# A three-part attention and feed-forward kernel: first loads taken apart, job slots and identity fillers changed

## The chip, the cores and the metric

One core of one Trainium2 chip runs the whole program. The metric is device time in microseconds (us), the median of three executions; lower is better. PE is the matmul engine (TensorE), PEld its weight load, DVE the VectorE, ACT the ScalarE, POOL the GpSimd and SP the SyncE, which here issues every transfer.

## The reference, cut to what matters

```python
# x: (4, 2048, 256); 16 heads of 16
x = x + 0.5 * ffn(layernorm(x))          # ffn: x @ W.T + b + (x @ V_r) @ C.T
x = x + attn(layernorm(x))
x = x + 0.5 * ffn(layernorm(x))
# attn
q, k, v = split(x @ W_attn)              # to (B, H, T, 16)
att = q @ k.T / 4, causal, -inf above the diagonal
att = polymax(att)     # x > 0: (x**2 + 1)/1000;  -100 <= x <= 0: (1 - x/100)/1000;  else 0
y = (att @ v) @ W_proj
```

## The kernel before, in words

The 8192 rows are 16 chunks of 512 (`NCH`, `CH`), four to each batch. Attention runs in 16 iterations (`ITERS`): one batch and one quad of four heads each. An iteration has 40 tiles (`TILES`, 128 keys by up to 512 queries), in four windows, one to each 512 queries (c = 0 to 3, of 4, 8, 12 and 16 tiles). A tile is two halves of two heads. PE makes a half's scores into `score`, DVE or ACT raises them into `rp` (and the linear part of a diagonal block into `lin`), POOL and ACT square them, and PE multiplies the tile with `vt` into `y_ps` three tiles later (`LAG`). What lies left of the diagonal for the linear part is one small product per 128 queries, `y_ps<-qT,st`, with a running state `st`; before, it opens a window, ahead of that window's first `values`.

The rest is jobs, in pieces on PE, each emptied from one of two banks by ACT or DVE. Stage A of a chunk: first norm, transposes `z1T`, `ffn`, second norm, transposes `z2T`. Stage B: `qT`, `k`, `v`, transposes `kT`, four `state` products; q and k are then split into three bf16 parts (`parts`, function `split`, on DVE for the first five chunks), stored to DRAM and loaded back into the layout that the score matmuls need. Stage C: `proj`, third norm, transposes `z3T`, `out`.

One line of slots sets the order on every engine: each engine goes through the slots in order and does what is put there. In iterations 1 to 15 each slot has one half, and tables such as `B_FULL` say at which of the iteration's 80 slots a job starts. Ahead of iteration 1 lie six stretches (36, 40, 40, 40, 44 and 48 slots) with stage A of chunk 0, then B of chunk c with A of chunk c + 1; the 80 halves of iteration 0 are spread over the later parts of the last four. I call the stretches S0 to S5 and all of it the warm-up. The slots of the whole warm-up number 248; how long a slot takes depends on what is in it.

Three lines show how the first iteration's inputs were made to wait:

```python
put(x.empty_at + 5, "kq", 0, x.chunk)      # behind the last kT job
all_stored(c + 1)                          # v, qT, parts and state of the chunk in DRAM
load_q(n, c, q_loaded[c]); load_k(n, c, k_loaded[c])
```

## Time and profile before

| what | us |
|---|---|
| median of 3 runs | 1920.25 (1919.88 to 1925.5) |
| the profiled execution, its own time | 1931.65 |
| its span | 1929.9 |
| PE busy | 1665.2 (86%) |
| DVE, ACT, POOL busy | 1361.7, 1363.2, 1326.5 |
| first copy of `y_ps` in iteration 1 | at 314.36 |

The span is what the views below divide up; it lies 1.75 us under that execution's own time. PE has the largest busy share, and its matmuls come at two speeds, which the same group of instructions shows by its duration. A last copy of `y_ps` at 302.28 marks the end of iteration 0, others at 404.86, 508.78 and 611.36 the ends of the next three.

### The profile page before, as it was taken

How to read it: one execution, taken by the hardware profiler on the slowest of the kernel's cores; microseconds unless marked ns; L12 is line 12 of the kernel's file. 1: busy time of each engine (PE TensorE's matmuls, PEld its weight loads, DVE VectorE, ACT ScalarE, POOL GpSimd, SP SyncE). 2: the span in 40 equal slices, each digit the busy share in tenths (PEclk: the TensorE clock that was granted, in tenths of full speed). 3: DMA queues.
4: the chain of work that ended last, by engine and by line, in shares of the span. 5: the costliest groups of instructions: out<-in, count | busy, mean ns of one | idle time of the engine just before them, and what ended most of it. 6: DMA issues, size and time to landing. Idle time of an engine off the chain costs nothing.

```text
span 1929.9 us, 66983 instructions
## 1 busy us (share of the span) xinstructions
PE 1665.2 (86%) x27158; PEld 814.6 (42%) x27158; DVE 1361.7 (71%) x3313; ACT 1363.2 (71%) x2178; POOL 1326.5 (69%) x1419
## 2 busy tenths in 40 slices
PE   4677789898989989898998989898898999898785
PEld 2343334343444435353443535344444444443342
DVE  1465677777777867778786777878676778787672
ACT  1244568787888777777877877777787788888561
POOL 3344558787778868777676877867677767686552
PEclk8888889999999999999999999999999999999897
DMA  2344433241424233341523334241324222323111
GB/s 75 124 128 129 114 106 108 83 110 49 133 67 136 85 103 95 99 132 50 159 66 111 87 106 128 71 135 57 117 86 130 86 72 80 82 73 78 49 37 59
DMA packets 155191, 183.14 MB, mean 95 GB/s; under 512 B 22012, under 2 KB 129660, under 8 KB 152836
## 3 DMA queue, kind: packets, MB, share of 16 engines
q1 hardware_dynamic: 154884, 178.82, 31.6%
q8 instruction: 221, 3.62, 0.8%
q14 instruction: 86, 0.70, 0.1%
HBM read 102.43 MB, written 76.30 MB: 93 GB/s over the span
## 4 chain that ended last, share of the span: by engine, by line
PE 54%; DVE 15%; ACT 12%; issue 8%; POOL 8%; DMA 2%; SPq 0%; ACTq 0%; POOLq 0%; DVEq 0%
PE y_ps L991 20%; PE score L991 16%; PE bank L991 14%; DVE rp L926 9%; ACT rp L831 4%; ACT rp L851 3%; PE bank L1017 3%; POOL rp L735 2%; POOL z L697 2%; ACT rp L847 2%; DVE lin L932 2%; DMA part_scratch<-parts 1%; POOL rp L710 1%; POOL parts L465 1%; DMA x1c<-x_scratch 1%
## 5 line engine op out<-in xcount | busy, mean ns | idle before, releaser
L926 DVE TENSOR_SCALAR rp<-score 128x512 f32<-128x512 f32 (+2 forms) x1728 | 944.1, 573 | 276.0 <-PE score L991 271.3
L991 PE MATMUL score<-qs,ks 96*32 96x512 bf16 (+3 forms) x10240 | 742.7, 354 | 137.8 <-DVE rp L926 74.6
L735 POOL TENSOR_TENSOR rp<-rp 128x1024 f32<-128x1024 f32 (+1 forms) x416 | 756.3, 1830 | 125.1 <-DVE rp L926 114.1
L831 ACT ACTIVATE rp<-score 128x512 f32<-128x512 f32 (+1 forms) x832 | 458.4, 592 | 267.8 <-PE score L991 266.2
L991 PE MATMUL y_ps<-rp,vt 128*16 128x512 f32 (+3 forms) x5120 | 597.8, 537 | 24.3 <-ACT rp L851 13.3
L991 PEld LDWEIGHTS score<-qs,ks 96*32 96x32 bf16 x10240 | 294.4, 96 | 547.9 <-DVE rp L926 266.8
L847 ACT ACTIVATE rp<-rp,rise 128x1024 f32<-128x1024 f32 (+1 forms) x416 | 462.6, 1144 | 1.7 <-POOL rp L710 1.7
L710 POOL TENSOR_SCALAR_AFFINE_SELECT rp<-rp 128x256 f32<-128x256 f32 (+1 forms) x384 | 185.2, 484 | 317.2 <-DVE rp L926 161.5
L851 ACT ACTIVATE rp<-rp 128x1024 f32<-128x1024 f32 (+2 forms) x224 | 291.1, 1305 | 131.4 <-DVE rp L926 66.0
L932 DVE SCALAR_TENSOR_TENSOR lin<-score,slope_mask 128x128 f32<-128x128 f32 x768 | 214.4, 279 | 0.0
L991 PEld LDWEIGHTS y_ps<-rp,vt 128*16 128x16 f32 x5120 | 134.4, 97 | 111.5 <-ACT rp L851 25.7
L991 PE MATMUL bank<-w_ffn,zT 128*32 128x256 f32 x2048 | 160.3, 401 | 5.4 <-ACT zT L791 5.4
L991 PE MATMUL bank<-w_qkv,z2T 128*32 128x256 f32 x2048 | 152.5, 388 | 11.2 <-ACT parts L808 11.2
L1017 PE MATMUL bank<-ident,z 128*128 128x128 f32 x384 | 72.7, 327 | 45.2 <-POOL z L697 42.9
L991 PE MATMUL y_ps<-lin,vt 128*16 128x128 f32 x2048 | 106.2, 276 | 0.0
L991 PEld LDWEIGHTS bank<-w_ffn,zT 128*32 128x32 f32 x2048 | 69.0, 115 | 79.6 <-issue 51.6
L697 POOL TENSOR_SCALAR z<-x,rstd_ln,shift_ln 128x256 f32<-128x256 f32 x128 | 72.6, 575 | 40.8 <-DVE shift_ln L885 39.3
L991 PEld LDWEIGHTS y_ps<-lin,vt 128*16 128x16 f32 x2048 | 61.5, 97 | 80.0 <-issue 67.8
L991 PEld LDWEIGHTS bank<-w_qkv,z2T 128*32 128x32 f32 x2048 | 67.3, 112 | 62.4 <-issue 28.0
L991 PE MATMUL bank<-w_out,y_c 128*32 128x256 f32 x1024 | 83.4, 400 | 11.8 <-DMA x1c<-x_scratch 11.8
L1017 PEld LDWEIGHTS bank<-ident,z 128*128 128x128 f32 x384 | 49.6, 164 | 88.5 <-issue 78.2
L697 POOL TENSOR_SCALAR z<-x_sb,rstd_ln,shift_ln 128x256 f32<-128x256 f32 x64 | 35.0, 558 | 68.2 <-DVE shift_ln L885 68.2
(78 smaller groups left out, 1360.0 us busy)
## 6 DMA issues: line engine op xcount, KB each, us to landing
part_scratch<-parts SPq DMA_DIRECT2D x16, 1536.0 KB, 7.5
qs<-part_scratch SPq DMA_DIRECT2D x384, 64.0 KB
ks<-part_scratch SPq DMA_DIRECT2D x384, 64.0 KB, 2.4
state_scratch<-st_new SPq DMA_DIRECT2D x16, 528.0 KB
st<-state_scratch SPq DMA_DIRECT2D x64, 132.0 KB
x_sb<-in_L_attn_x_dram SPq DMA_DIRECT2D x16, 512.0 KB, 4.4
x_scratch<-x SPq DMA_DIRECT2D x16, 512.0 KB, 5.4
qT_scratch<-qkT SPq DMA_DIRECT2D x16, 512.0 KB, 3.8
```

The lines of the kernel that those rows point to most:

```text
L465: ins = eng.tensor_tensor(parts[:, i, 2, :], rest[:], parts[:, i, 1, :], ALU.subtract)
L697: ins = pool.tensor_scalar(dst[:, i, :], src[:, i, :], rstd[k][:, i:i + 1], shift[k][:, i:i + 1], ALU.mult, ALU.add)
L710: pool.affine_select(out=block, in_=block, compare_op=ALU.is_ge, fill=fill, base=0, pattern=[[0, heads_in_it], [1, P]], channel_multiplier ...
L735: pool.tensor_tensor(half, half, half, ALU.mult).then_inc(squared["pool"], 1)
L831: nc.scalar.activation(rp[T % RP_BUFS][:, 2 + v, off:CH], score[H % S_BUFS][:, v, off:CH], ACT.Relu).then_inc(raised["act"], 1)
L847: nc.scalar.activation(part, part, ACT.Square, bias=rise[:]).then_inc(squared["act"], 1)
L851: nc.scalar.activation(whole, whole, ACT.Square).then_inc(squared["act"], 1)
L926: nc.vector.tensor_scalar(rp[T % RP_BUFS][:, 2 * u + v, off:CH], score[H % S_BUFS][:, v, off:CH], 0.0, RISE, ALU.max, ALU.add).then_inc(ra ...
L932: nc.vector.scalar_tensor_tensor(lin[D % L_BUFS][:, 2 * u + v, :], score[H % S_BUFS][:, v, off:off + P], ONE / SLOPE, slope_mask[:, 0, :], ...
L991: return nc.tensor.matmul(*args, start=start, stop=stop, skip_group_check=True)
L1017: ins = nc.tensor.transpose(dst[:, P * blk:P * blk + P], src[:, blk, P * i:P * i + P], ident[:])
```

## The change

Eight things are edited.

- Slots: the warm-up's stretches are 36, 40, 42, 39, 44 and 48 slots; halves of window c begin 33, 31, 31 and 33 slots into stretches S1 to S4 and are spread until the next window's begin. In stage B `kT` goes ahead of `v` and right behind `k`; the tables of the later iterations shift by 1 to 5 slots (`kT` part two from 52 to 57, `state` from 54, 56, 58 to 59, 61, 63).
- First transfers: for the first four chunks the half of q and the half of k that hold quad 0 are stored by themselves as soon as they are split, and quad 0 is loaded at once; v and the state's q go from SBUF to SBUF; the state is loaded late. The other halves of q and k follow in one store behind `kT`.
- `load_q` and `load_k` load only q and k; v, qT and the state have functions, semaphores and waits of their own.
- The state product closes a window instead of opening it, in pieces of 16 columns in place of 32, and the accumulation is started by the first `rp` product.
- Start: x is loaded first, four fills (`st_new`, `k_sb`, `qT`, `y_sb`) move from POOL to DVE, which also clears both `y_ps` banks, engines wait for the constants and weights that they need and not for all.
- Norms: ACT adds EPS as a bias of the square root, and the DVE addition is gone; the wait for the previous `z` moves to `aggregate`.
- Fillers: ahead of the transposes `z1T` and `z2T` of chunks 0 to 4, and of `proj` and `z3T` of the last chunk, PE does 48 matmuls of the identity by itself (12 times 4 strips of 128 columns) into the bank that the job is about to fill.
- Buffers freed in that way are waited for in `empty`.

```diff
-A_EARLY = {"z1T": (12, 13), "ffn": (14, 18), "z2T": (38, 39), "ln1": 0, "ln2": 22}
-B_EARLY = {"qT": (0, 2), "k": (4, 8), "v": (22, 26), "kT": (30, 32), "state": (31, 33, 34, 35)}
+A_EARLY = {"z1T": (12, 13), "ffn": (16, 20), "z2T": (38, 39), "ln1": 0, "ln2": 24}
+B_EARLY = {"qT": (4, 6), "k": (7, 8), "kT": (14, 15), "v": (26, 28), "state": (34, 35, 36, 37)}
+FILLERS = 12
+FILLED_UP = {(kind, c) for kind in ("z1T", "z2T") for c in range(CPB + 1)} | {("proj", NCH - 1), ("z3T", NCH - 1)}
+HALVES_AFTER = (33, 31, 31, 33)
+LENGTHS = (36, 40, 42, 39, 44, 48)
...
-    for c, (length, first) in enumerate(((40, 20), (40, 14), (44, 14), (48, 14))):
-        at = o.stretch(length, spread(first, length, 2 * (LAST[c] + 1 - FIRST[c])))
+    for c, length in enumerate(LENGTHS[1:]):
+        at = o.stretch(length)
+        o.stage(c, at, B_EARLY)
+        o.stage(c + 1, at, A_EARLY)
+        if c < CPB:
+            starts.append(at + HALVES_AFTER[c])
+    starts.append(o.n)
+    for c in range(CPB):
+        o.put_halves(spread(starts[c], starts[c + 1], 2 * (LAST[c] + 1 - FIRST[c])))
...
+                    if what == "first q":
+                        wait_emptied(sp, "qT", c, 0)
+                        sp.dma_start(qT[1:QD + 1, cols], qkT[0:QD, 0, :]).then_inc(qT_loaded[c], 16)
+                        sp.wait_ge(split_step, 12 * c + 3)
+                        sp.dma_start(part_d[c, :, 0, 0], parts[:, 0, :, :]).then_inc(first_q_stored, 16)
+                        sp.wait_ge(first_q_stored, (c + 1) * 16)
+                        load_q(0, c, q_loaded[c])
+                    if what == "first k":
+                        sp.wait_ge(split_step, 12 * c + 9)
+                        sp.dma_start(part_d[c, :, 1, 0], parts[:, KC, :, :]).then_inc(first_k_stored, 16)
+                        sp.wait_ge(first_k_stored, (c + 1) * 16)
+                        load_k(0, c, k_loaded[c])
...
-            act.wait_ge(const_ready, CONSTS)
+            def empty_weights():
...
+                if s == o.place["z1T", 0, 0].empty_at:
+                    empty_weights()
...
-            dve.wait_ge(const_ready, CONSTS)
+            nc.vector.memset(eps[:], EPS)
+            for k in range(KC):
+                nc.vector.memset(y_ps[k][:], 0.0).then_inc(y_cleared, 1)
+            nc.vector.memset(st_new[:], 0.0).then_inc(filled, 1)
+            nc.vector.memset(k_sb[:], 1.0).then_inc(filled, 1)
+            nc.vector.memset(qT[:], 1.0).then_inc(filled, 1)
+            nc.vector.memset(y_sb[0][:], 0.0).then_inc(filled, 1)
...
-                nc.vector.tensor_scalar(var[k][:], mv[k][:, :, 1], EPS, None, ALU.add).then_inc(var_done[k], 1)
...
+                if first and (kind, a) in FILLED_UP:
+                    for _ in range(FILLERS):
+                        strips(dst[:, 0:P], ident[:], ident[:])
...
-                    for m in range(NB):
-                        strips(y[:, P * m:P * m + P], st[:, NB * c + m, :], qT[:, CH * c + P * m:CH * c + P * m + P],
-                               start=m == 0, stop=False)
...
+                if t == LAST[c]:
+                    pe.wait_ge(qT_loaded[c], (n + 1) * 16)
+                    pe.wait_ge(st_loaded[c], (n + 1) * 16)
+                    for m in range(NB):
+                        for head in range(QH):
+                            ins = mm(y[STRIP * head:STRIP * head + HD, P * m:P * m + P],
+                                     st[:, NB * c + m, STRIP * head:STRIP * head + HD],
+                                     qT[:, CH * c + P * m:CH * c + P * m + P], start=False, stop=m == NB - 1)
```

On SP's queue, this is the stretch from the first qT store to the loads of chunk 0's q and k, before (`z` and `rp` above it hold weights at the start; `qkT`, `v_sb`, `st_new` and `parts` are the results that are stored):

```order
L595 DMA qT_scratch<-qkT 128x2x512
L590 DMA x_sb<-in_L_attn_x_dram 128x4x256
L591 DMA x_scratch<-x 128x4x256
L599 DMA v_scratch<-v_sb 128x1024
L608 DMA part_scratch<-parts 128x6144
L603 DMA state_scratch<-st_new 66x4x512
L516 DMA qs<-part_scratch 16x4x512 x6
L518 DMA qT<-qT_scratch 64x512
L521 DMA st<-state_scratch 66x4x128
L505 DMA ks<-part_scratch 16x4x512 x6
```

and the same place of the changed kernel:

```order
L668 DMA qT<-qkT 64x512
L670 DMA part_scratch<-parts 128x1536
L546 DMA qs<-part_scratch 16x4x512 x6
L642 DMA qT_scratch<-qkT 128x2x512
L676 DMA part_scratch<-parts 128x1536
L531 DMA ks<-part_scratch 16x4x512 x6
L660 DMA part_scratch<-parts 256x1x1536
L637 DMA x_sb<-in_L_attn_x_dram 128x4x256
L638 DMA x_scratch<-x 128x4x256
L646 DMA v_scratch<-v_sb 128x1024
L682 DMA vt<-v_sb 128x256
```

The loads of q and k now stand ahead of the next chunk's x, of the v store and of the state store; a quarter of `parts` goes out ahead of each.

On PE, this is the place where the very first half of iteration 0 stands, before:

```order
L1017 MATMUL bank<-ident,z 128x128 x8
L991 MATMUL bank<-w_ffn,zT 32x256 x24
L991 MATMUL score<-qs,ks 32x512 x8
L991 MATMUL bank<-w_ffn,zT 32x256 x8
L991 MATMUL score<-qs,ks 32x512 x8
```

and the same place of the changed kernel, with the filler of chunk 1's second transposes behind it:

```order
L1084 MATMUL bank<-w_ffn,zT 32x256 x32
L1084 MATMUL bank<-w_qkv,z2T 32x256 x32
L1084 MATMUL score<-qs,ks 32x512 x8
L1084 MATMUL bank<-v_sb,k_sb 32x64 x2
L1084 MATMUL bank<-v_sb,k_sb 2x64
L1084 MATMUL bank<-v_sb,k_sb 32x64 x2
...
L1084 MATMUL bank<-v_sb,k_sb 32x64 x2
L1084 MATMUL bank<-v_sb,k_sb 2x64
L1084 MATMUL bank<-v_sb,k_sb 32x64 x2
L1084 MATMUL bank<-v_sb,k_sb 2x64
L1084 MATMUL bank<-ident 32x128 x48
L1110 MATMUL bank<-ident,z 128x128 x8
```

The first half stood in the `ffn` of chunk 2; now it stands behind the `v` of chunk 0, one whole stretch earlier, ahead of the state products of chunk 0 and of the filler and the transposes of chunk 1.

Also on PE, the turn from one window to the next, in the warm-up: before,

```order
L991 MATMUL y_ps<-rp,vt 16x128 x4
L991 MATMUL y_ps<-lin,vt 16x128 x4
L991 MATMUL bank<-w_ffn,zT 32x256 x4
L991 MATMUL score<-qs,ks 32x512 x8
L991 MATMUL bank<-w_ffn,zT 32x256 x4
L991 MATMUL score<-qs,ks 32x512 x8
L991 MATMUL y_ps<-qT,st 32x128 x16
```

and now

```order
L1084 MATMUL score<-qs,ks 32x512 x8
L1084 MATMUL y_ps<-rp,vt 16x128 x4
L1084 MATMUL y_ps<-lin,vt 16x128 x4
L1084 MATMUL y_ps<-qT,st 16x128 x16
L1084 MATMUL score<-qs,ks 32x512 x16
L1084 MATMUL y_ps<-rp,vt 16x512 x4
```

The state product is 16 matmuls in both. It has moved up by two halves, and belongs to the window that ends.

## Rows read from the trace of the kernel before

**Rows 1.** The page: span, and busy time of each engine.

```profile
span 1929.9 us, 66983 instructions
PE 1665.2 (86%) x27158; PEld 814.6 (42%) x27158; DVE 1361.7 (71%) x3313; ACT 1363.2 (71%) x2178; POOL 1326.5 (69%) x1419
```

**Rows 2.** Stretches: length, busy PE, PEld, DVE, ACT, POOL, granted clock, DMA share, GB/s.

```profile
0.00:24.70 24.70, 6.89 (x20) 4.44 (x21) 2.30 (x11) 4.18 (x7) 10.67 (x24) 1.00 0.35 104
...
39.70:72.10 32.40, 24.26 (x344) 13.51 (x344) 13.49 (x39) 9.27 (x18) 8.25 (x14) 0.84 0.22 67
72.10:113.00 40.90, 30.92 (x456) 17.45 (x457) 23.82 (x60) 14.33 (x29) 17.59 (x25) 0.83 0.42 134
113.00:164.00 51.00, 37.99 (x608) 20.45 (x608) 30.13 (x80) 22.15 (x41) 24.53 (x32) 0.89 0.39 123
164.00:218.50 54.50, 42.67 (x652) 20.98 (x648) 34.14 (x84) 28.46 (x48) 26.10 (x30) 0.91 0.37 115
218.50:302.30 83.80, 70.60 (x1000) 32.14 (x1000) 59.19 (x134) 50.90 (x82) 43.45 (x47) 0.84 0.43 126
302.30:404.90 102.60, 92.15 (x1565) 44.32 (x1561) 78.12 (x189) 83.55 (x136) 79.97 (x83) 1.00 0.32 94
...
957.80:1069.90 112.10, 100.95 (x1704) 49.36 (x1700) 83.98 (x203) 85.18 (x139) 84.94 (x91) 0.98 0.34 102
1600.90:1691.50 90.60, 81.92 (x1359) 37.43 (x1352) 70.51 (x171) 75.16 (x117) 65.94 (x67) 1.00 0.29 77
```

**Rows 3.** Timeline of the start: begin, duration, instruction, idle time before and releaser.

```profile
12.26 0.40 PE L1003 MATMUL score<-ident,rp 128*32 128x128 f32 x1 [12.26 <-POOL bias_half L684]
...
22.40 2.17 POOL L697 TENSOR_SCALAR z<-x_sb,rstd_ln,shift_ln 128x256 f32<-128x256 f32 x4 [10.19 <-DVE shift_ln L885]
...
24.71 1.94 PE L1017 MATMUL bank<-ident,z 128*128 128x128 f32 x8 [4.84 <-POOL z L697]
...
27.43 6.34 PE L991 MATMUL bank<-w_ffn,zT 128*32 128x256 f32 x64 [0.78 <-ACT zT L791]
...
39.66 1.94 PE L1017 MATMUL bank<-ident,z 128*128 128x128 f32 x8 [5.88 <-POOL z L697]
```

**Rows 4.** Timeline of PE's queue in the warm-up.

```profile
55.23 1.06 PE L1017 MATMUL bank<-ident,z 128*128 128x128 f32 x8 [3.71 <-POOL z L697]
...
62.09 3.64 PE L991 MATMUL bank<-w_qkv,z2T 128*32 128x256 f32 x64
65.67 0.66 PE L1050 MATMUL bank<-ident,k_sb 128*128 128x128 f32 x4
66.54 0.64 PE L991 MATMUL bank<-v_sb,k_sb 128*32 128x64 f32 x24 [0.22 <-ACT v_sb L798]
...
98.20 0.62 PE L991 MATMUL score<-qs,ks 96*32 96x512 bf16 x8
```

**Rows 5.** Timeline of SP's queue and of ACT, 75 to 90 us.

```profile
75.24 0.36 SPq L608 DMA_DIRECT2D part_scratch<-parts  x1
...
83.31 2.70 SPq L516 DMA_DIRECT2D qs<-part_scratch  x6
...
81.70 0.60 ACT L807 ACTIVATE qkT<-bank 128x512 f32<-128x512 f32 x1 [7.78 <-DMA part_scratch<-parts]
```

**Rows 6.** DMA issues on the page: KB each and median us to landing.

```profile
qT_scratch<-qkT SPq DMA_DIRECT2D x16, 512.0 KB, 3.8
y_scratch<-y_sb SPq DMA_DIRECT2D x256, 32.0 KB, 1.7
```

**Rows 7.** Groups by form, iteration from 957.8 to 1069.9: count, busy us, mean ns, idle before.

```profile
L926 DVE TENSOR_SCALAR rp<-score 128x512 f32<-128x512 f32 x68 | 43.6, 682 | 7.1 <-PE score L991 6.9
...
L991 PE MATMUL score<-qs,ks 96*32 96x512 bf16 x448 | 37.5, 386 | 8.9 <-DVE rp L926 5.3 <-DVE lin L932 3.4
...
L991 PE MATMUL y_ps<-qT,st 66*32 66x128 f32 x128 | 4.2, 272 | 0.0
```

**Rows 8.** Timeline of the end.

```profile
1900.93 6.55 PE L991 MATMUL bank<-w_out,y_c 128*32 128x256 f32 x64 [6.08 <-DMA x1c<-x_scratch]
```

More of the change, by code:

```diff
@@ L155, in stage, with put_halves @@
                 self.jobs.append(Job(kind, chunk, i, at + start))
+    def put_halves(self, slots):
+        for s in slots:
+            assert s not in self.halves
+            self.halves[s] = self.next_half
+            self.next_half += 1
     def stretch(self, length, slots=()):
-        for s in slots:
-            self.halves[self.n + s] = self.next_half
-            self.next_half += 1
+        self.put_halves([self.n + s for s in slots])
         at = self.n
@@ L364, in build @@
         bank = [ps(f"bank{i}", [P, CH]) for i in range(2)]
-        w_loaded = sem("w_loaded")
+        ffn_loaded = sem("ffn_loaded")
+        bias_loaded = sem("bias_loaded")
+        qkv_loaded = sem("qkv_loaded")
+        out_loaded = sem("out_loaded")
+        ident_ready = sem("ident_ready")
+        filled = sem("filled")
+        y_cleared = sem("y_cleared")
+        first_q_stored = sem("first_q_stored")
+        first_k_stored = sem("first_k_stored")
         const_ready = sem("const_ready")
@@ L393, in build @@
         q_loaded = [sem(f"q_loaded{c}") for c in range(CPB)]
+        v_loaded = [sem(f"v_loaded{c}") for c in range(CPB)]
+        qT_loaded = [sem(f"qT_loaded{c}") for c in range(CPB)]
+        st_loaded = [sem(f"st_loaded{c}") for c in range(CPB)]
         qk_done = sem("qk_done")
@@ L569, in _ @@
                     put(x.empty_at + (2 if x.chunk < EARLY else 8), "parts", x.chunk)
-                    if x.chunk < CPB:
-                        put(x.empty_at + 5, "kq", 0, x.chunk)
+                if x.chunk < CPB:
+                    if (x.kind, x.i) == ("qT", 0):
+                        put(x.empty_at + 2, "first q", x.chunk)
+                    if (x.kind, x.i) == ("kT", 0):
+                        put(x.empty_at + 2, "first k", x.chunk)
+                    if (x.kind, x.i) == ("v", 1):
+                        put(x.empty_at + 1, "first v", x.chunk)
+                    if (x.kind, x.i) == ("state", NB - 1):
+                        put(x.empty_at + 7, "first st", x.chunk)
                 if (x.kind, x.i) == ("proj", 0):
@@ L615, in slot @@
+                    if what == "first st":
+                        c, = args
+                        sp.wait_ge(st_zero, 16 * BATCH)
+                        sp.wait_ge(st_stored, (c + 1) * 16)
+                        load_st(0, c, st_loaded[c])
                     if what == "q":
@@ L779, in _ @@
             nc.scalar.activation(cT[:], score[0][0:32, 0, DM:2 * DM], ACT.Copy).then_inc(setup_act, 1)
-            for k in range(KC):
-                act.wait_ge(setup_pe, 2 + k)
-                nc.scalar.activation(w_ffn[:, k, :], y_ps[k][:, 0:DM], ACT.Copy, scale=0.5).then_inc(setup_act, 1)
-            act.wait_ge(const_ready, CONSTS)
+            def empty_weights():
+                for k in range(KC):
+                    act.wait_ge(setup_pe, 2 + k)
+                    nc.scalar.activation(w_ffn[:, k, :], y_ps[k][:, 0:DM], ACT.Copy, scale=0.5).then_inc(setup_act, 1)
+                act.wait_ge(const_ready, CONSTS)
+                act.wait_ge(filled, FILLED)
             def empty(x):
@@ L858, in slot @@
                     if step == ROOT:
-                        act.wait_ge(var_done[k], chunk + 1)
-                        nc.scalar.activation(sd[k][:], var[k][:], ACT.Sqrt).then_inc(sd_done[k], 1)
+                        act.wait_ge(aggr_done[k], (chunk + 1) * NB)
+                        nc.scalar.activation(sd[k][:], mv[k][:, :, 1], ACT.Sqrt, bias=eps[:]).then_inc(sd_done[k], 1)
             for s in range(o.again):
+                if s == o.place["z1T", 0, 0].empty_at:
+                    empty_weights()
                 slot(s)
@@ L957, in _ @@
             for s in range(o.again):
+                if s == o.place["z1T", 0, 0].empty_at:
+                    dve.wait_ge(const_ready, CONSTS)
                 slot(s)
@@ L1035, in job @@
                         pe.wait_ge(c_loaded, (a + 1) * 32)
+                    if first and kind == "ffn" and a == 0:
+                        pe.wait_ge(setup_act, 4)
+                    if first and kind == "proj" and a == 0:
+                        pe.wait_ge(out_loaded, 16)
                     if first and kind in ("ffn", "out"):
@@ L1042, in job @@
                 if kind == "qT":
+                    if first and a == 0:
+                        pe.wait_ge(qkv_loaded, 16)
                     if first:
@@ L1098, in values @@
                     ins = mm(y[STRIP * head:STRIP * head + HD, off:CH], vt[:, kb, HD * head:HD * head + HD],
-                             rp[T % RP_BUFS][:, head, off:CH], start=False, stop=t == LAST[c])
+                             rp[T % RP_BUFS][:, head, off:CH], start=t == FIRST[c], stop=False)
                 if t in DIAG:
```

139 lines of the change are left out of this document (80 added, 59 removed).

## The prediction

> **What bounds the kernel now.** I read the page first: PE is busy 86% of the span, the other three 69 to 71% [rows 1], so PE's order and what it waits for decide. Then the stretches [rows 2]. Three kinds of time stand out. From 302.3 us on the kernel runs at a steady beat: 102.6 us for an iteration with stages A and B beside it, 112.1 with C as well, 90.6 with attention alone, and PE busy about 90% of each. The warm-up is another matter: from 39.7 to 302.3, 262.6 us, PE is busy only 75, 76, 74, 78 and 84% of the five stretches, and part of that is time at the lower clock: the granted clock there has means of 0.83 to 0.91, against 0.98 to 1.00 later. The third is the start, 24.7 us until the first transposes.
>
> In the start, every engine waits for POOL's work on the bias, which itself waits for the last weight: PE's first matmul is at 12.26. The first z is ready at 24.6, and the same eight transposes and the 64 products behind them take 1.94 and 6.34 us [rows 3], where later they take 1.06 and 3.64 [rows 4]. In the warm-up the timeline shows why PE is idle: no half may come until q, k, v and the state of the chunk are all stored and loaded, so the first score is at 98.20 [rows 4], 23 us behind the store of parts at 75.24, whose landing SP's loads (83.31) and ACT's next qT (7.78 us idle) both wait for [rows 5]. Until then PE has one chain to work on and nothing to fill its gaps; later the halves come in bunches between gaps.
>
> **The start.** x comes first, so the norm no longer waits for 12.2. DVE has its fills first: 6672 elements per partition over six. No row has a DVE fill. The bounds are nothing, if x lands behind them, and 9 us, at the 0.68 us that DVE takes to raise 512 columns of scores [rows 7]. A fill reads nothing, so I take 7, nearer to the upper end, and begin the statistics at 8. The Trainium skill (VectorE: DVE Perf Modes, "Zero memsets can be issued as uint32 (trn2)") says that a memset takes one cycle per element, which at the 0.96 GHz that the page gives is an estimate of 7.0 us; by it the term stays as it is. Then statistics and scales 4, POOL 2.2 [rows 3]: z at about 14. PE's twenty weight products are 6.89 us of its time [rows 2] with one step of ACT between; begun at 8 instead of 12.26, they end at 16. Then comes the filler. It is 96 records of 128 columns, where the 64 of 256 took 3.64: 2.7 us at the higher clock, and by 6.34 for 64, 4.8 at the lower. So the transposes start at 19 to 21 instead of 24.7. The 64 products behind them then run at the higher clock (2.7 less), and chunk 0's second transposes come at 32 instead of 39.7 (29 to 36): 7.7 gained.
>
> Why should a filler lift the clock? The rows give it: behind an idle gap of 5.88 the eight transposes take 1.94 [rows 3], behind one of 3.71 only 1.06 [rows 4]. A filler of 2.7 in a gap of 5.9 leaves 3.2. The Trainium skill (TensorE: Matmul & The Clock Gate, "What's actually happening") says the same in general, that the lower level is the default and activity releases it. Against it speaks Part 4 of that page, "PE-mode transpose", by which transposes don't count as such activity: if that held here, a filler which is followed only by transposes could be worth less, and each of the first four would cost its time and give back nothing.
>
> **The warm-up.** The same work in another order, so I sum it in two ways.
>
> First, by marginal price. Stages A and B of one chunk are PE work of four blocks of 3.64 (qT, k, v, ffn), two kT at 0.66, four state products at 0.64, and two sets of transposes at 1.06 [rows 4]: 20.5 us. C is some 8.3 (two blocks and one set of transposes) and adds 112.1 - 102.6 = 9.5 [rows 2], 1.13 for 1. An iteration with one A and B is 102.6, four more are 4 x 20.5 x 1.13 = 93, together 195. To that come S1, which has one half and cannot be filled (30 rather than 23: 7), six fillers in S2 to S4 at 2.7, of which I charge two thirds (11), and the splits, which in the warm-up are DVE's (3). Sum 216.
>
> Second, by PE's share. S1 to S5 have 24.26 + 30.92 + 37.99 + 42.67 + 70.60 us of PE, times their clocks 178 at the higher level [rows 2]; eight fillers add 22; at the 90% of an iteration that is 222. I take 219 between them, and iteration 0 ends at 32 + 219 = 251 instead of 302.3: 51 us less.
>
> Is q and k there in time? The kT of chunk 0 is now made some 11 slots before v is. Its split is 2.5 us of DVE, the store of 384 KB lands in 1.7 to 3.8 (32 KB and 512 KB, [rows 6]), SP then issues six loads in 2.7 [rows 5], and they land some 2 later (by the smaller of [rows 6]): about 11 us from kT to the first half, where PE has ffn and v, 7.3 us. So PE waits some 4 us at the first half, and the four state products and the second transposes of chunk 1 wait behind it. This is in S1's 30. Later stretches have halves of the window before in that place, and the wait is covered; without that cover it would be 4 us for each of three. SP itself stands still while it waits for each small store; behind it are the next x load and the stores of v and the state, needed a dozen slots later, so I cost that at nothing. If they came late, the next norm would be late by the same 2 to 4 us.
>
> **Later iterations.** The state product costs what it did, 4.2 us of records in an iteration [rows 7], with as many matmuls on as many columns, and moves past one tile's scores: nothing. DVE loses one small operation in each norm, and the shifted jobs spread what DVE and ACT empty over slots 49 to 63, where PE's 8.9 us of waiting for DVE in an iteration mostly lie [rows 7]. A gain is at most these 8.9 and a loss has no row as its bound; eleven iterations have such jobs. I take 0 for the likeliest, between -10 and +10 in all.
>
> **The end.** The last proj follows a gap of 6.08 us and takes 6.55 rather than 3.64 [rows 8]. Its filler lies in the gap: 2.9 gained if the clock holds, and about as much at z3T and out; at most 1 lost. I take 3.
>
> **Sum.** 51 + 3 = 54 us off the profiled 1931.65, so 1878 for that execution. It was 11.4 above the median of the runs; I carry the same difference, which gives 1920.25 - 54 = 1866.
>
> **Rivals.**
> (a) The warm-up fills badly. DVE has the splits and maxima there, halves stand in the order's way, the fillers delay scores instead of filling gaps, or each window's first half waits for its loads. For it: DVE has 59.19 us in the last stretch before and PE waits for it already. Against it: even then DVE is at 71% [rows 2]. If S2 to S5 reach only the 78% that PE had from 164 on, instead of 90, 200/0.78 = 256 us in place of 219, and the gain is 17: 1903. The page's rule on transposes, as a mechanism, comes in here: fillers without effect cost 2.7 each and leave the lower clock, 3.6 us for each of the four early sets, and the gain falls by some 20: 1886.
> (b) The later iterations gain as well. If the spread of the emptying takes 2.5 of the 8.9 us out of each of eleven, 28 more: 1838.
> (c) Slower. The shifted slots put state 61 and z2T 61 into one slot, both z3T into slot 69, and v with proj into 22 and 23, so PE waits for a bank to be emptied while DVE is behind in raising. It decides when it costs more than 54/11 = 4.9 us per iteration; at 6 it is 66, and 1932. Against it: the pairs alternate between the two banks and most gaps around them are of PE's making.
> (d) It does not do what it says: the first half waits for something that still comes at 90 us, for example in S1 for a blocked SP. Then only the start and the end are left, some 11 us: 1909.
>
> **How the numbers follow.** The forecast has 0.68, with a range of its own from 1845 to 1886; (a) 0.15, (b) 0.07, (c) 0.06, (d) 0.04. 1866 is the time of the first. The range leaves out (c) and half of (b): 1838 to 1902. Within 0.3% (6 us) is about what a measurement cannot tell from no change; only edges of (c) and (d) lie there, so same has 0.03, slower 0.05, faster 0.92.
>
> **What the profile after would show.** Right: PE's first matmul at 7 to 9 us, the second transposes of chunk 0 near 32, the first score at 55 to 60, the fourth copy of y_ps (end of iteration 0) near 251, a granted clock above 0.95 from 70 us on, and iterations still of 102 to 104 and 111 to 113 us. Wrong: the fourth copy after 270 with PE waiting for DVE's rp or for loads of q and k, transposes of 1.9 us behind fillers, or an iteration of more than 114.

## The result, and the profile after

The changed kernel takes 1789.11 us, the median of four runs (1787.53 to 1792.33), against 1922.88 (1919.88 to 1926.72) for the kernel before on the same chip: a ratio of 0.9305 [0.928, 0.9331]. The forecast was 1866, with a range down to 1838; the gain is 134 us where 54 were expected. The profiled execution took 1787.62.

The page after, span and busy time of each engine (compare [rows 1]):

```profile
span 1785.9 us, 69303 instructions
PE 1636.3 (92%) x28310; PEld 866.6 (49%) x28310; DVE 1327.8 (74%) x3272; ACT 1363.1 (76%) x2178; POOL 1318.3 (74%) x1415
```

The stretches after, with the columns of [rows 2]:

```profile
0.00:19.60 19.60, 11.33 (x117) 8.49 (x117) 7.95 (x17) 4.27 (x7) 8.54 (x23) 1.00 0.44 132
...
31.00:64.90 33.90, 27.53 (x553) 17.18 (x553) 18.20 (x46) 10.59 (x22) 10.91 (x18) 0.95 0.44 141
64.90:101.70 36.80, 31.52 (x667) 21.20 (x664) 27.07 (x66) 16.95 (x33) 20.57 (x29) 1.00 0.51 157
101.70:148.80 47.10, 41.77 (x853) 24.90 (x849) 33.34 (x77) 24.10 (x40) 25.37 (x28) 0.96 0.46 143
148.80:201.40 52.60, 46.14 (x836) 25.48 (x834) 35.19 (x84) 30.87 (x50) 27.54 (x32) 0.97 0.35 114
201.40:265.90 64.50, 55.18 (x897) 27.42 (x900) 48.58 (x109) 42.63 (x71) 37.09 (x43) 0.97 0.35 111
265.90:361.20 95.30, 90.26 (x1568) 45.20 (x1564) 75.02 (x188) 83.69 (x136) 79.60 (x83) 1.00 0.35 103
868.70:970.00 101.30, 97.48 (x1708) 52.07 (x1700) 80.07 (x201) 85.45 (x140) 84.87 (x92) 1.00 0.37 109
```

The end of iteration 0 moved from 302.3 to 265.9: 36.4 us, where I had forecast 51. Iterations 1 to 11 went from 102.6 to 95.3 us each without C and from 112.1 to 101.3 with it, 102.6 us in all, where I had forecast nothing. The rest (iterations 12 to 15 and the end) gave 5. So the larger half of the gain lies in a place that I had priced at 0, and PE is now busy 95 and 96% of such an iteration, not 90.

The timeline of PE's start after, with the columns of [rows 3]:

```profile
7.54 0.37 PE L1096 MATMUL score<-ident,rp 128*32 128x128 f32 x1 [7.54 <-DMA z<-in_L_ffn_W_dram]
...
15.06 4.60 PE L1084 MATMUL bank<-ident 128*32 128x128 f32 x96
19.59 1.09 PE L1110 MATMUL bank<-ident,z 128*128 128x128 f32 x8
21.60 3.66 PE L1084 MATMUL bank<-w_ffn,zT 128*32 128x256 f32 x64 [0.92 <-ACT zT L871]
25.05 2.83 PE L1084 MATMUL bank<-ident 128*32 128x128 f32 x96
30.93 1.09 PE L1110 MATMUL bank<-ident,z 128*128 128x128 f32 x8 [3.04 <-POOL z L774]
...
58.30 0.62 PE L1084 MATMUL score<-qs,ks 96*32 96x512 bf16 x8 [1.43 <-DMA ks<-part_scratch]
```

The start is as I drew it: first matmul at 7.54, a filler of 4.60 and then one of 2.83 (so the clock of 1.00 given for the first stretch cannot be right: the durations decide), transposes of 1.09 and 64 products in 3.66 behind it, second transposes at 30.93, first score at 58.30. On SP's queue the small store of k and the loads of chunk 0 stand so close together:

```profile
50.20 0.37 SPq L676 DMA_DIRECT2D part_scratch<-parts  x1
53.02 2.68 SPq L531 DMA_DIRECT2D ks<-part_scratch  x6
```

DVE's fills took this long (two of its six rows of fills):

```profile
1.15 1.02 DVE L958 MEMSET y_ps<- 128x512 f32 x2
2.59 1.76 DVE L959 MEMSET st_new<- 66x2048 f32 x1 [0.41 <-issue]
```

### The profile page after: what moved, and what is told of

Read it like the earlier page. It is cut to its first block, busy times and chain, and to the rows that moved or that the text cites. A ratio compares the mean times of both kernels' runs of the same rounds, so it can differ in the third digit from the quotient of the medians.

```text
span 1785.9 us, 69303 instructions
## 1 busy us (share of the span) xinstructions
PE 1636.3 (92%) x28310; PEld 866.6 (49%) x28310; DVE 1327.8 (74%) x3272; ACT 1363.1 (76%) x2178; POOL 1318.3 (74%) x1415
## 4 chain that ended last, share of the span: by engine, by line
PE 59%; DVE 15%; ACT 11%; issue 6%; POOL 5%; DMA 2%; SPq 2%; ACTq 0%; POOLq 0%; DVEq 0%
PE y_ps L1084 21%; PE bank L1084 18%; PE score L1084 16%; DVE rp L1017 9%; ACT rp L915 4%; PE bank L1110 3%; ACT rp L931 2%; POOL rp L812 2%; DVE lin L1023 2%; DMA x1c<-x_scratch 2%; ACT rp L935 1%; DVE bnst_ln L1042 1%; ACT lin L921 1%; POOL z L774 1%; SPq L531 1%
## 5 line engine op out<-in xcount | busy, mean ns | idle before, releaser
L1084 PE MATMUL score<-qs,ks 96*32 96x512 bf16 (+3 forms) x10240 | 729.4, 350 | 54.0 <-DVE lin L1023 22.4
L915 ACT ACTIVATE rp<-score 128x512 f32<-128x512 f32 (+1 forms) x832 | 463.1, 602 | 210.3 <-PE score L1084 208.1
L1084 PEld LDWEIGHTS score<-qs,ks 96*32 96x32 bf16 x10240 | 306.2, 96 | 431.6 <-DVE rp L1017 142.7
L1084 PEld LDWEIGHTS y_ps<-rp,vt 128*16 128x16 f32 x5120 | 143.8, 96 | 117.4 <-issue 38.9
L1084 PE MATMUL bank<-w_ffn,zT 128*32 128x256 f32 x2048 | 154.8, 387 | 4.5 <-ACT zT L871 2.9
L1084 PEld LDWEIGHTS y_ps<-lin,vt 128*16 128x16 f32 x2048 | 65.1, 96 | 74.3 <-issue 62.4
L1084 PE MATMUL bank<-w_out,y_c 128*32 128x256 f32 x1024 | 88.5, 390 | 13.1 <-DMA x1c<-x_scratch 13.1
L921 ACT ACTIVATE lin<-score 128x128 f32<-128x128 f32 x256 | 80.7, 315 | 0.0
L1110 PE MATMUL bank<-ident,z 128*128 128x128 f32 x384 | 61.0, 292 | 19.5 <-POOL z L774 18.7
L1084 PE MATMUL bank<-z2T,w_qkv 128*32 128x512 f32 x512 | 68.1, 605 | 2.3 <-ACT z2T L871 2.3
```

Of the source, the lines that this page charges most:

```text
L915: nc.scalar.activation(rp[T % RP_BUFS][:, 2 + v, off:CH], score[H % S_BUFS][:, v, off:CH], ACT.Relu).then_inc(raised["act"], 1)
L921: nc.scalar.activation(lin[D % L_BUFS][:, 2 + v, :], score[H % S_BUFS][:, v, off:off + P], ACT.Copy, scale=SLOPE, bias=ONE).then_inc(lin_d ...
L1084: return nc.tensor.matmul(*args, start=start, stop=stop, skip_group_check=True)
L1110: ins = nc.tensor.transpose(dst[:, P * blk:P * blk + P], src[:, blk, P * i:P * i + P], ident[:])
```

## Where the later iterations' time went: DVE standing still in three places

I had read DVE by its busy share. These are groups by form of DVE in the kernel before, in the iteration of [rows 7] (957.8 to 1069.9): count, busy, mean ns, idle before them and what ended it.

```profile
L885 DVE SCALAR_TENSOR_TENSOR shift_ln<-mv_ln,rstd_ln 128x4 f32<-128x4 f32 x3 | 3.8, 1278 | 0.1
L912 DVE TENSOR_TENSOR st_add<-bank,smask 66x256 f32<-66x256 f32 x4 | 1.7, 421 | 3.6 <-PE bank L991 2.2 <-POOL st_new L759 1.5
L903 DVE SCALAR_TENSOR_TENSOR x<-bank,x1c 128x512 f32<-128x512 f32 x2 | 1.4, 692 | 3.2 <-PE bank L991 3.2
L897 DVE TENSOR_TENSOR x<-bank,x_sb 128x512 f32<-128x512 f32 x2 | 1.4, 692 | 1.4 <-PE bank L991 1.3
L908 DVE TENSOR_TENSOR x<-bank,x 128x512 f32<-128x512 f32 x2 | 1.4, 692 | 4.1 <-PE bank L991 4.1
```

And the same groups after, 868.7 to 970.0:

```profile
L976 DVE SCALAR_TENSOR_TENSOR shift_ln<-mv_ln,rstd_ln 128x4 f32<-128x4 f32 x3 | 1.8, 616 | 0.1
L1003 DVE TENSOR_TENSOR st_add<-bank,smask 66x256 f32<-66x256 f32 x4 | 1.7, 415 | 1.1 <-PE bank L1084 1.1
L994 DVE SCALAR_TENSOR_TENSOR x<-bank,x1c 128x512 f32<-128x512 f32 x2 | 1.4, 692 | 1.9 <-PE bank L1084 1.9
L999 DVE TENSOR_TENSOR x<-bank,x 128x512 f32<-128x512 f32 x2 | 1.4, 692 | 1.5 <-PE bank L1084 1.5
L988 DVE TENSOR_TENSOR x<-bank,x_sb 128x512 f32<-128x512 f32 x2 | 1.4, 692 | 0.8 <-PE bank L1084 0.8
```

DVE raises two thirds of the scores (1728 of the 2560 pieces on the page), in order with all else that it does. Whatever holds it there holds the next scores on PE. Three things held it: the idle time ahead of emptying a `state` product (3.6 us, now 1.1), that ahead of emptying `proj`, `ffn` and `out` (3.2 + 1.4 + 4.1 = 8.7, now 4.2), and `shift_ln`, an operation on four elements that took 3.8 us in three (now 1.8). Together 16.1 before and 7.1 after: 9.0 of the 10.8 us by which this iteration is shorter. The first two are idle time of an engine that was not the bound by its share, the third counts as busy. In iteration 2, summed in the same way, it is 9.0 and 3.9, 5.1 of the 8.7. Over iterations 1 to 11 the three come to 155.6 us before and 66.8 after, where the length fell by 102.5.

A part of the gain is the clock: its mean was 0.98 in six of iterations 1 to 11 before, and 1.00 in all eleven after. It is not the main part: in the kernel of experiment 17 it was 1.00 in all eleven too, and they took 71 us more than in the changed kernel.

**Emptying ahead of raising.** A job's last piece is emptied by DVE in the slot where PE computes it, ahead of that slot's raising. In an even slot PE has the scores of a half, then a whole tile's `values`, and then the piece. This is the kernel before in such a slot, a timeline of PE and DVE:

```profile
471.15 0.40 PE L991 MATMUL score<-qs,ks 96*32 96x512 bf16 x4 [0.40 <-DVE lin L932]
471.37 1.04 PE L991 MATMUL y_ps<-rp,vt 128*16 128x512 f32 x8
472.23 0.52 PE L991 MATMUL bank<-v_sb,k_sb 128*32 128x64 f32 x18
472.90 0.42 DVE L912 TENSOR_TENSOR st_add<-bank,smask 66x256 f32<-66x256 f32 x1 [1.31 <-PE bank L991]
473.25 0.68 DVE L926 TENSOR_SCALAR rp<-score 128x512 f32<-128x512 f32 x1
473.98 0.40 PE L991 MATMUL score<-qs,ks 96*32 96x512 bf16 x4 [0.69 <-DVE rp L926]
```

The scores that end at 471.55 are raised only from 473.25 on: DVE idles for 1.31 us until the product is there, which stands behind them and behind the values, empties it, and PE then waits 0.69 us for DVE. In an odd slot there are no values and it is mostly ACT that raises; here is the changed kernel with a state product in such a slot:

```profile
425.30 0.61 PE L1084 MATMUL score<-qs,ks 96*32 96x512 bf16 x8
425.73 0.51 PE L1084 MATMUL bank<-v_sb,k_sb 128*32 128x64 f32 x18
425.81 1.14 ACT L915 ACTIVATE rp<-score 128x512 f32<-128x512 f32 x2
426.41 0.42 DVE L1003 TENSOR_TENSOR st_add<-bank,smask 66x256 f32<-66x256 f32 x1 [0.61 <-PE bank L1084]
426.46 1.18 PE L1084 MATMUL y_ps<-rp,vt 128*16 128x512 f32 x8
```

The tables moved `state` from slots 48, 54, 56, 58 to 49, 59, 61, 63, and the emptying of `out` from 74 and 78 to 75 and 79. `proj` and `ffn` were emptied in odd slots before and are still; that the idle time ahead of them fell too (3.2 to 1.9 and 1.4 to 0.8) is not explained by the kind of slot.

**An operation of four elements held by POOL.** `shift_ln` takes 0.2 us when it is alone. In the kernel of experiment 1 (the changed one with the old tables) it takes 3.31 and ends at 435.65; the product's last matmul ended at 435.17, so here it is `shift_ln` that keeps the emptying and the raise behind it waiting:

```profile
431.89 3.74 POOL L812 TENSOR_TENSOR rp<-rp 128x1024 f32<-128x1024 f32 x2
432.34 3.31 DVE L976 SCALAR_TENSOR_TENSOR shift_ln<-mv_ln,rstd_ln 128x4 f32<-128x4 f32 x1
432.82 1.05 PE L1084 MATMUL score<-qs,ks 96*32 96x512 bf16 x16
433.70 1.03 PE L1084 MATMUL y_ps<-rp,vt 128*16 128x512 f32 x8
434.56 0.50 PE L1084 MATMUL bank<-v_sb,k_sb 128*32 128x64 f32 x18
435.58 0.41 DVE L1003 TENSOR_TENSOR st_add<-bank,smask 66x256 f32<-66x256 f32 x1
435.91 0.67 DVE L1017 TENSOR_SCALAR rp<-score 128x512 f32<-128x512 f32 x1
```

POOL had begun two squarings at 431.89 and ends at 435.63. This is the rule, not a coincidence: in the twenty kernels of this study 607 executions of `shift_ln` took over 0.25 us, and every one began while POOL was at work and ended within 0.03 us of the end of a POOL operation, typically 0.02 behind it. Most of them met a squaring of `rp`; 49 met only POOL's selects (0.4 us), and were 0.25 to 0.42 us long. The other 353 took 0.16 to 0.25 us, and where one of them began beside a POOL operation, that had at most 0.24 us left. It can sit through several in a row. The kernel of experiment 16, with C, shows it at its worst; POOL, DVE and PE in one timeline:

```profile
937.11 3.74 POOL L812 TENSOR_TENSOR rp<-rp 128x1024 f32<-128x1024 f32 x2
937.30 4.69 DVE L976 SCALAR_TENSOR_TENSOR shift_ln<-mv_ln,rstd_ln 128x4 f32<-128x4 f32 x1
939.20 0.63 PE L1084 MATMUL score<-qs,ks 96*32 96x512 bf16 x8
940.82 1.15 POOL L492 TENSOR_TENSOR parts<-rest,parts 128x512 bf16<-128x512 f32 x1
941.91 0.68 DVE L1017 TENSOR_SCALAR rp<-score 128x512 f32<-128x512 f32 x1
942.93 0.62 PE L1084 MATMUL score<-qs,ks 96*32 96x512 bf16 x4 [3.10 <-DVE lin L1023]
```

POOL's three operations end at 941.97, DVE's at 941.99, and PE then has waited 3.10 us. `shift_ln` is DVE's only operation in these iterations that reads two tensors from SBUF; all the others, which read PSUM or one tensor, keep their usual length (the raise of 512 columns is never over 0.69 us in iterations 1 to 11 of the changed kernel, `lin` never over 0.29). The Trainium skill (SBUF — State Buffer, "SBUF: two separate sides") gives a reason: a DVE operation with two SBUF inputs and a GpSimd operation that reads SBUF take turns at a shared pair of ports for the whole instruction, and the loser fully blocks. The traces agree, with 0.2 us alone and up to 4.69 behind POOL.

## The experiments

The ratio is against the kernel before on the same chip, whose median was 1922 to 1928 us beside the different experiments; compare by it rather than by the times. The last columns are the mean length of an iteration without C (1 to 3) and with it (4 to 10), first score to first score.

| run | median us | ratio [95%] | without C | with C |
|---|---|---|---|---|
| kernel before | 1922.88 | 1 | 103.0 | 111.6 |
| changed kernel | 1789.11 | 0.9305 [0.928, 0.9331] | 95.3 | 101.2 |
| 1 old tables | 1896.12 | 0.9834 [0.9817, 0.985] | 103.5 | 111.4 |
| 2 old norm | 1798.58 | 0.9331 [0.9311, 0.935] | 95.8 | 101.5 |
| 3 state opens | 1782.62 | 0.9244 [0.9228, 0.9259] | 95.6 | 100.4 |
| 4 no fillers | 1782.35 | 0.9248 [0.9226, 0.9269] | 95.3 | 101.3 |
| 5 only B table | 1866.55 | 0.9713 [0.9685, 0.9741] | 98.6 | 109.3 |
| 6 only state | 1861.13 | 0.968 [0.9655, 0.9705] | 100.9 | 107.5 |
| 7 only kT | 1866.82 | 0.9707 [0.968, 0.9734] | 100.5 | 108.3 |
| 8 four st_add | 1873.38 | 0.9754 [0.9721, 0.9787] | 102.1 | 109.0 |
| 9 before, new tables | 1822.13 | 0.9485 [0.9459, 0.9512] | 95.5 | 100.7 |
| 10 both of 3 and 4 | 1775.08 | 0.9244 [0.9219, 0.9269] | 95.1 | 100.1 |
| 11 only A table | 1876.73 | 0.9768 [0.9744, 0.9791] | 101.0 | 109.1 |
| 12 old warm-up slots | 1805.91 | 0.9401 [0.9361, 0.9441] | 95.3 | 101.2 |
| 13 short POOL split | 1879.37 | 0.976 [0.9741, 0.9779] | 101.4 | 109.7 |
| 14 short DVE | 1887.23 | 0.9795 [0.9777, 0.9812] | 102.7 | 109.6 |
| 15 short ACT | 1877.93 | 0.9758 [0.9738, 0.9778] | 101.2 | 109.2 |
| 16 A and B tables | 1839.19 | 0.9563 [0.9533, 0.9592] | 95.3 | 106.8 |
| 17 state odd, close | 1866.45 | 0.97 [0.9673, 0.9727] | 101.3 | 108.0 |
| 18 state even, spread | 1886.49 | 0.9802 [0.9781, 0.9823] | 102.4 | 110.0 |

**1. The changed kernel with the old tables.**

```diff
-A_FULL = {"z1T": (32, 33), "ffn": (36, 40), "z2T": (61, 63), "ln1": 10, "ln2": 45}
-B_FULL = {"qT": (0, 7), "k": (8, 12), "v": (16, 20), "kT": (45, 57), "state": (49, 59, 61, 63)}
-C_FULL = {"proj": (22, 26), "ln3": 30, "z3T": (69, 69), "out": (72, 76)}
+A_FULL = {"z1T": (32, 34), "ffn": (38, 42), "z2T": (61, 63), "ln1": 8, "ln2": 45}
+B_FULL = {"qT": (0, 6), "k": (8, 12), "v": (16, 20), "kT": (46, 52), "state": (48, 54, 56, 58)}
+C_FULL = {"proj": (24, 28), "ln3": 32, "z3T": (65, 67), "out": (71, 75)}
```

> The changed kernel with the job tables of the later iterations (A_FULL, B_FULL, C_FULL) as before; warm-up, norms, state product and fillers stay. Theory 1 (the shifted jobs of iterations 1 to 11 gave the 103 us that these iterations gained): about 1875 to 1890, with an iteration back at 102 us without C and 112 with C. Theory 2 (the norm without its DVE addition and with its wait moved) and theory 3 (the state product at the window's end): within 10 us of the changed kernel's 1789.

Measured: 107 us slower than the changed kernel by the times, 102 by the ratios, and its iterations are nearly those of the kernel before. The three tables carry the whole of the later gain.

**2. The norm as before.**

```diff
-                        nc.scalar.activation(sd[k][:], mv[k][:, :, 1], ACT.Sqrt, bias=eps[:]).then_inc(sd_done[k], 1)
+                        nc.scalar.activation(sd[k][:], var[k][:], ACT.Sqrt).then_inc(sd_done[k], 1)
...
+                nc.vector.tensor_scalar(var[k][:], mv[k][:, :, 1], EPS, None, ALU.add).then_inc(var_done[k], 1)
```

> The changed kernel with the norm as before: DVE adds EPS in an operation of its own that waits for the four aggregates, and the wait for the previous z stands ahead of the reciprocal. Theory 2: 1860 or more, since DVE's wait inside the norm would stop the raising of scores behind it. Theory 1 and 3: 1789 to 1797, three small operations per iteration.

Measured: 0.9331, its interval overlaps that of the changed kernel. At most a few us, if anything. In its one profile iteration 1 begins at 264.3 instead of 257.3, and iterations 1 to 11 take 3.6 us more in all.

**3. The state product at the opening of a window, from iteration 1 on.**

```diff
-                if t == LAST[c]:
+                if t == LAST[c] and n == 0:
...
+                if t == FIRST[c] and n > 0:
```

> The changed kernel with the state product at the opening of a window, in pieces of 32 columns, as before, in iterations 1 to 15 (iteration 0 keeps it at the end). Theory 3: 1850 or more. Theory 1 and 2: 1785 to 1795; the attention-only iterations say that the place is worth under 1 us each (91.4 after against 90.6 before).

Measured: about 0.6% faster by the ratio, 6.5 us by the times. From iteration 1 on, closing a window with the state product costs some 0.4 to 0.8 us in an iteration. "Nothing", as I had it, was a small error of the other sign. Whether it helps in iteration 0, where the state comes late, no run shows: this kernel has it at the end there too.

**4. No fillers.**

```diff
-FILLERS = 12
+FILLERS = 0
```

> The changed kernel without fillers. My sum charged eleven us for them in the warm-up against 2.7 to 3.6 given back at each of the first sets and 3 at the end: 1780 to 1800. If they lift the clock for long stretches, 1810 or more, with transposes of 1.9 us at 19, 31 and 45 us; if they only cost, 1775.

Measured: also about 0.6% faster by the ratio, 6.8 us by the times. The kernel without fillers, timeline of its start and of its end:

```profile
15.23 1.97 PE L1110 MATMUL bank<-ident,z 128*128 128x128 f32 x8
17.97 6.00 PE L1084 MATMUL bank<-w_ffn,zT 128*32 128x256 f32 x64 [0.78 <-ACT zT L871]
...
1752.19 5.88 PE L1084 MATMUL bank<-w_out,y_c 128*32 128x256 f32 x64 [7.69 <-DMA x1c<-x_scratch]
```

The fillers do what they are said to: with them the same lines take 1.09, 3.66 and, at the end, 5.02. But transposes and ffn of chunk 0 begin at 15.23 and not at 19.59, which pays for both, and each later filler costs 2.8 in a stretch where PE is short of time: iteration 1 begins at 248.4 without them and at 257.3 with them. At the end they give 1.9 us from proj to the last matmul (21.07 to 19.15).

**9. The kernel before with the three new tables and nothing else.**

```diff
-B_FULL = {"qT": (0, 6), "k": (8, 12), "v": (16, 20), "kT": (46, 52), "state": (48, 54, 56, 58)}
+B_FULL = {"qT": (0, 7), "k": (8, 12), "v": (16, 20), "kT": (45, 57), "state": (49, 59, 61, 63)}
```

(A_FULL and C_FULL likewise.)

> The kernel before with the three tables of the later iterations new (A_FULL, B_FULL, C_FULL) and nothing else. If the tables do the same without the rest of the change: 1922 - 107 = 1815 (1808 to 1825), iterations of 95.3 and 101. If they need the norm without its addition, or the state product at the window's end: 1840 or more.

Measured: 1822.13, 100 us under the kernel before. Neither the norm nor the place of the state product is needed for it.

**10. Experiments 3 and 4 together.**

> The changed kernel without fillers and with the state product at the opening of a window in iterations 1 to 15: each alone was 11 us faster than the changed kernel by its ratio. If they add: ratio 0.918 to 0.921, about 1767. If both do the same thing (PE's work in the same places): 0.924.

Measured: 1775.08, the fastest kernel here, 14 us under the changed one. By ratio it is level with each of the two alone; the kernel before ran at 1922 beside it and at 1928 beside them, so the ratios do not tell whether the two gains add.

**12. The warm-up's slots of before, with the new stores and start.**

```diff
-LENGTHS = (36, 40, 42, 39, 44, 48)
+    for c, (length, first) in enumerate(((40, 20), (40, 14), (44, 14), (48, 14))):
```

(and A_FIRST, A_EARLY and B_EARLY of before.)

> The changed kernel with the warm-up's slots as before (stretches, places of the halves, A_FIRST, A_EARLY, B_EARLY); the first stores, the start and the fillers stay new. If the earlier and evenly spread halves give the warm-up's gain: the first score at 80 or later, the end of iteration 0 at 290 or more, and 1805 to 1820. If the smaller first stores and the start are the gain: 1789 to 1797.

Measured: 1805.91, and iteration 1 begins at 272.7, where the changed kernel has 257.3 and the one before 293.7. The first score falls back to 84.59, and iteration 0 ends at 281.3, not at 290. So the slots are worth 15 us of the 36, and the start, the stores apart and the fillers the other 21; each of my two cases had one of them alone.

**5, 11, 16, 6 and 7. One table, two tables, one row of a table.** From experiment 1: only the new B_FULL; only the new A_FULL; both; only `state` at 49, 59, 61, 63; only `kT` at 45 and 57. The edits of the last two:

```diff
-"state": (48, 54, 56, 58)
+"state": (49, 59, 61, 63)
...
-"kT": (46, 52)
+"kT": (45, 57)
```

> The changed kernel with A_FULL and C_FULL as before, so that of the three tables only B_FULL (qT, kT, state) is new. Theory 1a (the crowd in slots 46 to 60, where kT, four state products, the splits on POOL and the second norm meet, is what was relieved): most of the 107 us stay, 1800 to 1825. Rival 1b (ffn, z1T, proj, norms and out matter as much): 1840 to 1870.

> The changed kernel with B_FULL and C_FULL as before, only A_FULL new (z1T, ffn and the first norm of the iteration). B_FULL alone gave 23 of 107 us. If the parts help only together, because each of them takes work out of slots 44 to 60 and the slowest of the others remains: 1870 to 1890. If A alone has the missing 80: 1815 to 1830.

> The changed kernel with A_FULL and B_FULL new and C_FULL as before. In iterations without C: 95.3 as in the changed kernel. With C: if A and B add up as they do without it (2 and 2 us alone), 107, ratio 0.955; if C's own shift matters little, 102 and 0.935.

> All three tables old, but the state products at 49, 59, 61, 63 instead of 48, 54, 56, 58. If the state products' chain (PE, DVE, POOL's addition, next DVE) is what stops PE behind DVE: 1825 to 1850. If kT's second part with its splits is: 1880 to 1896.

> All three tables old, but kT at 45 and 57 instead of 46 and 52. State chain theory: 1880 to 1896. kT and splits theory (ACT's two copies, POOL's two subtractions of 1.16 us away from slots 54 and 55): 1825 to 1850.

Measured: by the ratios, of the 102 us, 13 with A alone, 23 with B alone, 52 with both, so they do not add. `state` alone and `kT` alone each give as much as all of B (0.968 and 0.9707 against 0.9713). That is a miss of both theories of 6 and 7: each had one of the two doing nearly all and the other next to nothing. In the traces `kT` seems to work through `shift_ln`: in iteration 2 the longer of its two executions takes 0.34 us, where experiment 1 has 3.31, while the idle time ahead of the emptied `state` products even rises, from 4.4 to 5.0, and the iteration falls from 103.6 to 100.5 (a part of that is the clock, 0.97 and 1.00). Experiment 16 separates C: without C its iterations are those of the changed kernel (95.3), with it they are 5.6 longer. The groups by form of DVE in its iteration 868.6 to 975.7:

```profile
L976 DVE SCALAR_TENSOR_TENSOR shift_ln<-mv_ln,rstd_ln 128x4 f32<-128x4 f32 x3 | 5.3, 1770 | 0.1
...
L999 DVE TENSOR_TENSOR x<-bank,x 128x512 f32<-128x512 f32 x2 | 1.4, 692 | 4.1 <-PE bank L1084 4.1
```

`shift_ln` takes 3.5 us more than in the changed kernel, and the two emptyings of `out`, here in even slots, have 2.6 more idle time ahead of them: 6.1, in an iteration that is 6.2 longer, first score to first score. Here C's table is worth what these two say.

**8. Four buffers for `st_add`**, with the old tables.

```diff
-        st_add = [sb(f"st_add{i}", [QR, DM]) for i in range(2)]
+        st_add = [sb(f"st_add{i}", [QR, DM]) for i in range(4)]
...
-                    if a * NB + i >= 2:
+                    if a * NB + i >= 4:
```

> All three tables old, with four st_add buffers instead of two, so that DVE does not wait for POOL's addition before it masks the next state product. If DVE's wait for POOL (1.5 us of idle in the iteration's trace) with the raising of scores queued behind it is the mechanism: 1840 to 1875. If POOL's and DVE's own load in these slots is: 1885 to 1896.

Measured: 0.9754, by the ratio 15 us under experiment 1. POOL's part of the wait (1.5 us before) can be taken away so, and is the smaller part.

**13, 14 and 15. Is it too much work rather than its order?** With the old tables, each leaves work out on one engine.

> The changed kernel with the old tables (as e1_old_tables, ratio 0.983) where POOL's two subtractions of each split, 1.16 us each, are done on 8 columns instead of 512 in iterations 1 to 15, so that work is left out and the output is not the reference's. POOL theory (in slots 48 to 60 POOL is the engine that holds everybody up): the iterations fall to 96 to 98 without C, ratio 0.94 to 0.95. Rival theories (ACT, or DVE itself): ratio 0.97 to 0.98.

> The changed kernel with the old tables where DVE's masking of the state products and its maxima of q and k work on 8 columns in iterations 1 to 15 (3.6 us of DVE less per iteration, work left out). DVE theory: ratio 0.945 to 0.955. POOL theory: 0.97 to 0.98.

> The changed kernel with the old tables where ACT's part of the splits and its two copies of kT work on 8 columns in iterations 1 to 15 (4.8 us of ACT less per iteration, work left out). ACT theory: ratio 0.945 to 0.955. POOL theory: 0.97 to 0.98.

Measured: 0.976, 0.9795 and 0.9758, so 4 to 8 parts in a thousand, where the order of the jobs is worth 53. The load that these edits take away is not the cause, on any of the three engines. In the first, the shorter splits also change when POOL's work meets `shift_ln`, which falls from 3.3 to 2.3.

**17 and 18. Odd or even, close or spread.** With the old tables, `state` alone at other slots:

```diff
-"state": (48, 54, 56, 58)
+"state": (49, 55, 57, 59)    # 17
+"state": (50, 60, 62, 64)    # 18
```

> All three tables old, state products at 49, 55, 57, 59 instead of 48, 54, 56, 58: one slot later each, spacing as before. In an even slot PE does a half's scores, then a tile's values, then the state product, and DVE empties that product before it raises the same half; in an odd slot there are no values and mostly ACT raises. Parity theory: at least two thirds of e6's 30 us, ratio 0.968 to 0.975. Spacing theory (the products must be spread and come later): 0.980 to 0.984.

> All three tables old, state products at 50, 60, 62, 64: spread and late as in e6 (49, 59, 61, 63), but in even slots. Parity theory: little of e6's gain, ratio 0.978 to 0.984. Spacing theory: ratio 0.966 to 0.972.

Measured, as a square: even and close 0.9834, odd and close 0.970, even and spread 0.9802, odd and spread 0.968. Odd slots gain 0.012 to 0.013 either way, spreading 0.002 to 0.003. Ahead of the four emptyings in iteration 2 DVE is idle for 4.4, 3.0, 7.5 and 2.6 us in that order. Even and spread has 3 us more of it than even and close and is still not slower, because its `shift_ln` meets POOL at another moment: 0.6 us, against 3.3.

**What the square left open, as the traces have it.** Here is what DVE stands for in iteration 7, in the three places, beside the iteration's length:

| kernel | shift_ln | idle ahead of st_add | ahead of proj, ffn, out | sum | iteration |
|---|---|---|---|---|---|
| before | 3.8 | 3.6 | 8.8 | 16.2 | 112.1 |
| 1 | 4.2 | 3.8 | 7.6 | 15.6 | 110.3 |
| 5 | 5.8 | 1.1 | 7.6 | 14.5 | 109.5 |
| 18 | 1.5 | 6.8 | 7.6 | 16.0 | 109.5 |
| 11 | 4.5 | 3.8 | 7.7 | 16.0 | 108.5 |
| 7 | 3.6 | 3.0 | 7.6 | 14.2 | 108.3 |
| 6 | 4.5 | 2.4 | 6.8 | 13.7 | 107.5 |
| 16 | 5.3 | 1.1 | 7.7 | 14.1 | 107.1 |
| changed | 1.8 | 1.1 | 4.2 | 7.1 | 100.9 |
| 3 | 1.6 | 1.1 | 3.4 | 6.1 | 100.2 |

Over all twenty kernels the sum and the length go together with a correlation of 0.98 in iteration 7 and 0.94 in iteration 2, at 0.95 and 1.12 us of iteration per us of standing. Much of that is two groups, seven kernels that stand 6.0 to 7.2 us in iteration 7 and thirteen that stand 13.7 to 16.2; among the thirteen alone it is 0.69. It also suggests why the parts do not add: new state slots bring the emptying forward, but while `shift_ln` holds DVE for 3 us at the same place, the raising is late all the same. This part is read from traces; that `shift_ln` by itself costs what it stands for was not tried by an edit of its own.

**What the three places do not hold: A's part.** Over iterations 1 to 11, the new B_FULL takes 35.8 us out of the length and 33.8 out of the sum (experiments 1 and 5), and the new C_FULL 42.3 and 49.2 (16 and the changed kernel). But the new A_FULL takes out 24.7 us of length while the sum rises by 3.3 (1 and 11), or 26.9 while it falls by 4.0 (5 and 16). In iteration 2 the kernels of 5 and 16 stand nearly alike, 4.2 and 3.9 us, and yet take 98.6 and 95.3: the 3.3 us are lost between the 25th and the 49th half, where `z1T` and `ffn` are. So about a quarter of the later gain has a cause that is shown (the table) and a mechanism that stays open.

## Why the prediction was wrong

**The start: right.** First matmul 7.54 (7 to 9), fills of about 7 us (7), filler 4.60 (4.8) and 2.8 (2.7), first transposes 19.59 (19 to 21), second ones 30.93 (32). The memset at one cycle per element, as the Trainium skill (VectorE: DVE Perf Modes, "Zero memsets can be issued as uint32 (trn2)") has it, gives an estimate of 2.1 us for the 2048 elements that took 1.76; the trace is somewhat faster, and the term stood. Part 4 of TensorE: Matmul & The Clock Gate in the Trainium skill, by which I let the fillers be worth nothing as a rival, did not decide: transposes behind fillers took 1.09 us, and without them 1.97 (experiment 4). The first filler's 4.6 us were in my sum; what I did not set beside it is the start without it, where the transposes begin at 15.23. Over the whole run the fillers are a net loss (experiment 4).

**The first score: right.** 58.30 for 55 to 60, waiting 1.43 us for k's load where I had 4.

**The warm-up: half wrong.** S1 to S5 took 234.9 us and not 219. PE's busy time there by its clock is 196 (I had 178 and 22 for fillers, 200), so the work was right; the share was not. I took the 90% of an iteration [rows 2] for it, and it was 196/235 = 84%, between that and the 78% of rival (a). What PE waited for from 31.0 to 265.9: 15.5 us for one of its two banks to be emptied by ACT or DVE, 8.2 for DVE to raise scores or make `lin`, 6.9 for POOL's z and 1.4 for the load of k. I had priced no wait for a bank there. The charge for the fillers was not too small: I took 11 us, and without them iteration 1 begins 8.9 us earlier.

**Later iterations: this step failed.** "A gain is at most these 8.9 ... I take 0." Both halves of it were wrong. The bound came from one group's idle time, PE's ahead of `score` [rows 7]. The chain of waits also runs through the weight load, which in that iteration waited 17.0 us for DVE's `rp` and waits 7.1 now; so the gain of 10.8 us with C is above my bound. And I took 0 because the state product costs the same and DVE "loses one small operation", which argues from work, when what the tables change is what stands ahead of what. Rival (b) had the direction and 28 us of it; the runs show 102.6, 3.7 times that. What they show in place of my step is DVE standing still, idle ahead of small emptyings and held in `shift_ln`: 155.6 us of it over iterations 1 to 11 before and 66.8 after, with A's part of the gain left open. Rival (c) feared the shifted slots for bank waits; in these iterations none is to be seen.

**The end: nearly right.** 1.9 us between the fillers and none, where I had 3: proj took 5.02, not 3.64, so only part of it ran at the higher clock.
